# Seven normalisations: halves added on GpSimd, mean squares by token on the partitions

## The chip, the cores and the metric

The kernel runs on one core of one Trainium2 chip. A core has TensorE (PE, matrix products into the 8 banks of PSUM; its weight loads are listed apart as PEld), VectorE (DVE), ScalarE (ACT), GpSimd (POOL) and the DMA queues, SyncE's (SP) among them. Each engine works through its own queue in order; they meet through semaphores. The metric is the device time of one execution in microseconds; lower is better. All data are fp32.

## The reference

One pass over x of shape (4, 256, 32, 32): a convolutional gate, windowed attention, then two layers of fast weights, a pattern layer, head-mixing attention and a mixture of experts, on 4096 tokens of 256 channels. Between them stands this, seven times in what runs here:

```python
def layer_norm(x, g, b):
    m = jnp.mean(x, axis=-1, keepdims=True)
    v = jnp.mean(jnp.square(x - m), axis=-1, keepdims=True)
    return (x - m) * jax.lax.rsqrt(v + EPS) * g + b
```

`_ln_t` is the same without g and b. The axis is that of the 256 channels; EPS is 1e-5.

## The kernel before

The program is a row of stages; each is a block with one instruction stream for each engine and ends in a barrier of all engines (end_stage). Activations lie channels on partitions: a tensor of [128, 2, 4096], where the 2 (CH) are the halves of the 256 channels and 4096 (T) the tokens. So a mean over channels is a sum over partitions, which PE does with a matrix of 1/256 ("ones"), and over two halves.

norm_stage (L338 to L468) runs as ln2, lnf0, lnff, lnf1, ln3, ln4 and ln5, in this order; lnf0, lnff and lnf1 have a gain and a shift. (ln3s stands in a branch of pattern_layer that isn't taken.) It works on NG = 8 groups of GROUP = 512 tokens. For a group g:

- mean(g), L368: two matmuls of 512 columns (one a half) with "ones" into bank g % 3. Every row of the bank then holds the mean.
- centre(g), DVE, L441: dst = src - mean, 128x1024.
- square(g), ACT, L412: squares into sq, three buffers.
- squares(g), PE, L376: two matmuls of 512 columns with a slice of pick, a matrix with one column of 1/256 in it, so that group g's sum falls on row g % 4 of bank 3 or 4. Four groups (HALF) fill a [4, 512] tile.
- root(b), ACT, L416, and invert(b), DVE, L445: square root and reciprocal on [4, 512], once for each half of the groups.
- spread(g), PE, L386: one matmul of 512 columns that takes row g % 4 of rstd to all 128 partitions, bank 5 + g % 3.
- scale(g), DVE: dst times that bank, in one instruction (L451) or, with a gain, in two (L455). move(g), ACT, L424: the shift, two instructions.

The order is written out by hand. PE: means two ahead of squares, groups 0 to 3; then squares of groups 4 to 7, each followed by a spread of groups 0 to 3; then the spreads of 4 to 7. DVE: six centrings, the first reciprocal, two centrings, four scalings, the second reciprocal, four scalings. ACT: five squares, a root, three squares, a root, the shifts. POOL only fills constants (L357 to L360). An fp32 matmul is two MATMUL records in the trace.

The prediction also names rows of other stages: L704 and its neighbours (fast_weight_stage, 32x32 and 128-column tiles), L1755 (matmuls of one moving column), L2119 (of eight), L1215 and L1784 (transposes of 128 columns), L655 and L1692 (additions on POOL), L106 (an activation of one element a partition).

## Time and profile before

| | |
|---|---|
| time, median of 3 runs | 5374.98 us (5358.56 to 5387.59) |
| the profiled execution | 5375.21 us, span 5373.4 us |
| PE busy | 4530.5 us (84%) |
| DVE busy | 2972.1 us (55%) |
| ACT busy | 2152.0 us (40%) |
| POOL busy | 831.7 us (15%) |
| L368, means, PE | 128 records from X and 96 from Y |
| L445, reciprocals of [4, 512], DVE | 14, about 3.34 us each |

The span is from the first to the last instruction that the profile shows; the rest of the time lies around it. Busy shares are averages over stages with different limits, so what a change of one stage is worth is read in that stage. PEclk is the clock that was granted to TensorE, as a share of its full 2.4 GHz; it has two levels, 1.0 and 0.5, and a mean of a window lies between them.

### The profile page before, as it was taken

How to read it: one execution, taken by the hardware profiler on the slowest of the kernel's cores; microseconds unless marked ns; L12 is line 12 of the kernel's file. 1: busy time of each engine (PE TensorE's matmuls, PEld its weight loads, DVE VectorE, ACT ScalarE, POOL GpSimd, SP SyncE). 2: the span in 40 equal slices, each digit the busy share in tenths (PEclk: the TensorE clock that was granted, in tenths of full speed). 3: DMA queues.
4: the chain of work that ended last, by engine and by line, in shares of the span. 5: the costliest groups of instructions: out<-in, count | busy, mean ns of one | idle time of the engine just before them, and what ended most of it. 6: DMA issues, size and time to landing. Idle time of an engine off the chain costs nothing. (4 is left out here: it accounts for less than half of the span.)

```text
span 5373.4 us, 139944 instructions
## 1 busy us (share of the span) xinstructions
PE 4530.5 (84%) x57100; PEld 2834.8 (53%) x57101; DVE 2972.1 (55%) x5849; ACT 2152.0 (40%) x4091; POOL 831.7 (15%) x2139
## 2 busy tenths in 40 slices
PE   3679898887997888897688886799999999984995
PEld 1237777773436777774355554354454545433663
DVE  3444444453024544454488886488686877852343
ACT  1133223232123333331466664277575766721221
POOL 0000000000000000000355553011111111104012
PEclk7788878798998988898899998899999999985997
DMA  1000000000000000000100000000000000006123
GB/s 42 2 7 3 3 3 3 3 3 18 0 0 9 4 3 3 3 4 3 38 1 1 1 1 0 10 1 1 1 0 1 0 1 1 0 3 217 61 84 101
DMA packets 47552, 85.70 MB, mean 16 GB/s; under 512 B 7121, under 2 KB 38129, under 8 KB 46065
## 3 DMA queue, kind: packets, MB, share of 16 engines
q1 hardware_dynamic: 40944, 61.84, 3.3%
q0 software_dynamic: 6144, 16.79, 1.0%
q8 instruction: 401, 6.57, 0.5%
q14 instruction: 63, 0.51, 0.0%
HBM read 45.05 MB, written 33.55 MB: 15 GB/s over the span
## 5 line engine op out<-in xcount | busy, mean ns | idle before, releaser
L1775 PE MATMUL psum<-hm_ex,hm_mix 128*128 128x512 f32 x1024 | 510.4, 621 | 42.3 <-ACT hm_Aq L1855 38.3
L1841 ACT ACTIVATE hm_ex<-psum,hm_nm 128x1024 f32<-128x1024 f32 x256 | 285.6, 1116 | 299.4 <-DVE hm_nm L1899 299.4
L1775 PEld LDWEIGHTS psum<-hm_ex,hm_mix 128*128 128x128 f32 x1024 | 175.6, 191 | 352.5 <-issue 344.8
L1914 DVE COPY hm_A<-psum 128x1024 f32<-128x1024 f32 x256 | 312.9, 1222 | 51.5 <-PE psum L1784 47.9
L1909 DVE TENSOR_SCALAR_CACHE_REDUCE hm_plus<-hm_Aq,hm_cbcol,hm_sums 128x1024 f32<-128x1024 f32 x256 | 340.5, 1330 | 0.0
L1899 DVE TENSOR_REDUCE hm_nm<-psum 128x1 f32<-128x1024 f32 x256 | 311.0, 1215 | 13.5 <-PE psum L1763 13.5
L1784 PEld LDWEIGHTS psum<-K,hm_Aq 128*128 128x128 f32 x2048 | 236.6, 140 | 150.0 <-issue 145.4
L957 DVE TENSOR_TENSOR fw_M<-fw_M,psum 128x256 f32<-128x256 f32 x256 | 107.8, 421 | 348.1 <-PE psum L728 345.6
L1846 ACT ACTIVATE hm_junk<-hm_Aq 128x1024 f32<-128x1024 f32 x256 | 270.6, 1057 | 30.3
L1763 PE MATMUL psum<-hm_kt,hm_qd 64*32 64x512 f32 x4096 | 280.1, 606 | 0.0
L1321 ACT ACTIVATE pt_signs<-pt_acts,pt_tb 128x1024 f32<-128x1024 f32 (+1 forms) x224 | 227.6, 1018 | 116.1 <-POOL pt_tb L1188 95.0
L1784 PE MATMUL psum<-K,hm_Aq 128*128 128x128 f32 x2048 | 266.6, 273 | 5.7 <-DVE hm_A L1914 5.6
L1855 ACT ACTIVATE hm_Aq<-psum 128x1024 f32<-128x1024 f32 x256 | 259.5, 1014 | 11.1 <-PE psum L1775 11.1
L704 PE MATMUL psum<-fw_rk,fw_ntx 128*128 128x64 f32 x2048 | 253.9, 278 | 0.0
L704 PEld LDWEIGHTS psum<-fw_rk,fw_ntx 128*128 128x128 f32 x2048 | 247.4, 194 | 6.7
L715 PE MATMUL psum<-fw_M,fw_pkt 128*32 128x128 f32 x1024 | 185.2, 310 | 74.3 <-issue 38.1
L669 PE MATMUL psum<-fw_w,fw_stage 128*128 128x512 f32 (+1 forms) x512 | 226.6, 593 | 22.9 <-POOL fw_stage L650 19.0
L655 POOL TENSOR_TENSOR fw_loff<-fw_bg,K 128x256 f32<-128x256 f32 x64 | 57.0, 890 | 1163.2 <-DVEq L937 1163.2
L1235 PE MATMUL psum<-pt_w_proc,pt_keptT 128*128 128x512 f32 x512 | 225.6, 599 | 10.3 <-ACT pt_keptT L1306 10.3
L2226 ACT ACTIVATE ex_ht<-psum,ex_b 128x128 f32<-128x128 f32 x320 | 91.2, 368 | 324.6 <-PE psum L2158 241.6
L1692 POOL TENSOR_TENSOR hm_mix<-hm_kron,hm_rinv 128x128 f32<-128x128 f32 x256 | 102.1, 399 | 664.8 <-DVE hm_rinv L1904 664.8
L1405 DVE TENSOR_SCALAR_CACHE_REDUCE pt_over<-pt_acts,pt_tb 128x1024 f32<-128x1024 f32 (+1 forms) x96 | 101.7, 1097 | 161.9 <-POOL pt_tb L1188 161.9
(379 smaller groups left out, 9044.6 us busy)
## 6 DMA issues: line engine op xcount, KB each, us to landing
ex_rows_in<-ex_zero SPq DMA_DIRECT2D x2, 5120.0 KB, 24.8
ex_xs<-ex_rows_in SPq DMA_DIRECT2D x80, 128.0 KB
ex_rows_out<-ex_ys SPq DMA_DIRECT2D x80, 128.0 KB, 1.7
ex_w<-in_ex_w SPq DMA_DIRECT2D x2, 4096.0 KB
X<-in_x SPq DMA_DIRECT2D x2, 2048.0 KB, 12.5
out_y<-X SPq DMA_DIRECT2D x2, 2048.0 KB, 9.0
ff_w<-in_ff_w SPq DMA_DIRECT2D x2, 1024.0 KB, 5.8
pt_w_proc<-in_pt_proc SPq DMA_DIRECT2D x1, 2048.0 KB, 7.6
```

The source lines that it names most:

```text
L669: mm = pe.matmul(bank[b][:, 0:hi - lo], stage[:, h, :], w[:, h, lo:hi], start=(h == 0), stop=(h == CH - 1))
L704: mm = pe.matmul(bank[2][:, 64 * n:64 * n + 64], by[:, n, :], of(n), start=True, stop=True)
L1321: act.activation(signs[:, u, 0:n], acts[:, lane(j), u, 0:n], ACT.Sign, bias=tb[:, lane(j), u, 0:1], accum_out=tb[:, lane(j), u, 1:2]).then ...
L1763: mm = pe.matmul(bank[2 * u + c][32 * pr:32 * pr + 32, :], qd[64 * c:64 * c + 64, u, pr, :, :].rearrange("p j n -> p (j n)"), kt[64 * c:64 ...
L1775: mm = pe.matmul(bank[4 + c], mix[:, u, :], ex[:, u, 512 * c:512 * c + 512], start=True, stop=True)
L1784: mm = pe.transpose(bank[6 + m // 4][:, P * (m % 4):P * (m % 4) + P], Aq[:, u, P * m:P * m + P], k.const("ident"))
L1841: act.activation(ex[:, u, :], flat2(psum[:, 2 * u:2 * u + 2, :]), ACT.Exp, bias=nm[:, u:u + 1], accum_out=rsum[:, u:u + 1]).then_inc(s_ex, 1)
L1846: act.activation(junk[:, :], Aq[:, u, :], ACT.Square, accum_out=ssq[:, bass.ds(b * TI + i, 1)]).then_inc(s_sq, 1)
L1855: act.activation(Aq[:, u, :], flat2(psum[:, 4:6, :]), ACT.Copy).then_inc(s_cp, 1)
L1899: dve.tensor_reduce(nm[:, u:u + 1], flat2(psum[:, 2 * u:2 * u + 2, :]), AX.X, ALU.max, negate=True).then_inc(s_nm, 1)
L1909: dve.tensor_scalar(plus[:, :], Aq[:, u, :], cbcol[:, :], sums[:, :], ALU.add, ALU.add, accum_out=sums[:, :]).then_inc(s_run, 1)
L1914: dve.tensor_copy(A[:, :, :, QT_ * t:QT_ * t + QT_], flat2(psum[:, 6:8, :]).rearrange("p (m g n) -> p m g n", m=MT, g=HEADS)).then_inc(s_a ...
```

## The change

POOL now adds the two halves of the channels before PE sums over partitions: halves(g) = src[0] + src[1], two buffers, so that mean(g) is one matmul of 512 columns; and sqs(g) = sq[0] + sq[1], two buffers. The mean squares are then taken with the tokens on the partitions: four matmuls a group, each with 128 tokens of sqs as the stationary operand and one column of "ones" moving, give a [128, 4] tile in bank 3 + g % 2. Root and reciprocal work on [128, 4], once for each group. spread(g) is four matmuls with one column of rstd, read 128 times, as the stationary operand, and the identity (128 columns) moving; each gives 128 of the group's 512 columns. pick is gone. The order is one loop over t on each engine: PE mean(t), squares(t-2), spread(t-3); ACT square(t), root(t-2), move(t-4); DVE centre(t), invert(t-2), scale(t-3); POOL sum_halves(t+2), sum_squares(t). New waits: mean on halves, squares on sqs and std, square on sqs (two buffers of sq instead of three), root on its own group's squares, invert on its own group's root; scale waits for square(g).

```diff
@@ -338,67 +338,79 @@
 def norm_stage(k, name, src, dst, gain=None, shift=None):
     nc = k.nc
-    HALF = NG // 2
+    PARTS = GROUP // P
     with ExitStack() as ctx:
-        sq = k.sb(f"{name}_sq", [P, 3, CH, GROUP], ctx)
-        std = k.sb(f"{name}_std", [HALF, 2, GROUP], ctx)
-        rstd = k.sb(f"{name}_rstd", [HALF, 2, GROUP], ctx)
-        eps = k.sb(f"{name}_eps", [P, 1], ctx)
-        pick = k.sb(f"{name}_pick", [P, 2 * HALF - 1], ctx)
-        s_zero, s_eps, s_mean, s_cen, s_sq, s_msq, s_std, s_rstd, s_bc, s_out, s_shift = (
-            k.sem(f"s_{name}_{n}") for n in "zero eps mean cen sq msq std rstd bc out shift".split())
+        sb = lambda n, s: k.sb(f"{name}_{n}", s, ctx)
+        halves = sb("halves", [P, 2, GROUP])
+        sq = sb("sq", [P, 2, CH, GROUP])
+        sqs = sb("sqs", [P, 2, GROUP])
+        std = sb("std", [P, NG, PARTS])
+        rstd = sb("rstd", [P, NG, PARTS])
+        eps = sb("eps", [P, 1])
+        s_eps, s_halves, s_mean, s_cen, s_sq, s_sqs, s_msq, s_std, s_rstd, s_bc, s_out, s_shift = (
+            k.sem(f"s_{name}_{n}") for n in "eps halves mean cen sq sqs msq std rstd bc out shift".split())
         bank = k.bank
         at = lambda ap, g: ap[:, :, GROUP * g:GROUP * g + GROUP]
         both = lambda ap: ap.unsqueeze(1).broadcast_to([P, CH, GROUP])
         with nc.Block() as block:
             @block.gpsimd
             def _(pool):
-                pool.memset(eps[:, :], EPS)
-                pool.memset(pick[:, :], 0.0).then_inc(s_zero, 1)
-                pool.wait_ge(s_zero, 1)
-                pool.memset(pick[:, HALF - 1:HALF], 1.0 / C).then_inc(s_eps, 1)
+                def sum_halves(g):
+                    if g >= 2:
+                        pool.wait_ge(s_mean, g - 1)
+                    pool.tensor_tensor(halves[:, g % 2, :], at(src, g)[:, 0, :], at(src, g)[:, 1, :],
+                                       ALU.add).then_inc(s_halves, 1)
+                def sum_squares(g):
+                    pool.wait_ge(s_sq, g + 1)
+                    if g >= 2:
+                        pool.wait_ge(s_msq, g - 1)
+                    pool.tensor_tensor(sqs[:, g % 2, :], sq[:, g % 2, 0, :], sq[:, g % 2, 1, :],
+                                       ALU.add).then_inc(s_sqs, 1)
+                pool.memset(eps[:, :], EPS).then_inc(s_eps, 1)
+                sum_halves(0)
+                sum_halves(1)
+                for g in range(NG):
+                    if g + 2 < NG:
+                        sum_halves(g + 2)
+                    sum_squares(g)
             @block.tensor
             def _(pe):
                 def mean(g):
+                    pe.wait_ge(s_halves, g + 1)
                     if g >= 3:
                         pe.wait_ge(s_cen, g - 2)
-                    for h in range(CH):
-                        mm = pe.matmul(bank[g % 3], k.const("ones"), src[:, h, GROUP * g:GROUP * g + GROUP],
-                                       start=(h == 0), stop=(h == CH - 1))
-                    mm.then_inc(s_mean, 1)
+                    pe.matmul(bank[g % 3], k.const("ones"), halves[:, g % 2, :], start=True, stop=True).then_inc(s_mean, 1)
                 def squares(g):
-                    pe.wait_ge(s_sq, g + 1)
-                    r = g % HALF
-                    for h in range(CH):
-                        mm = pe.matmul(bank[3 + g // HALF][0:HALF, :], pick[:, HALF - 1 - r:2 * HALF - 1 - r],
-                                       sq[:, g % 3, h, :], start=(r == 0 and h == 0),
-                                       stop=(r == HALF - 1 and h == CH - 1))
+                    pe.wait_ge(s_sqs, g + 1)
+                    if g >= 2:
+                        pe.wait_ge(s_std, g - 1)
+                    for q in range(PARTS):
+                        mm = pe.matmul(bank[3 + g % 2][:, q:q + 1], sqs[:, g % 2, P * q:P * q + P], k.const("ones")[:, 0:1],
+                                       start=True, stop=True)
                     mm.then_inc(s_msq, 1)
                 def spread(g):
-                    pe.wait_ge(s_rstd, g // HALF + 1)
+                    pe.wait_ge(s_rstd, g + 1)
                     if g >= 3:
                         pe.wait_ge(s_out, g - 2)
-                    r = g % HALF
-                    pe.matmul(bank[5 + g % 3], k.const("ident")[0:HALF, r:r + 1].broadcast_to([HALF, P]),
-                              rstd[:, g // HALF, :], start=True, stop=True).then_inc(s_bc, 1)
-
-                mean(0)
-                mean(1)
-                pe.wait_ge(s_eps, 1)
-                for g in range(HALF):
-                    mean(g + 2)
-                    squares(g)
-                mean(6)
-                mean(7)
-                for g in range(HALF):
-                    squares(HALF + g)
-                    spread(g)
-                for g in range(HALF):
-                    spread(HALF + g)
+                    for q in range(PARTS):
+                        mm = pe.matmul(bank[5 + g % 3][:, P * q:P * q + P], rstd[:, g, q:q + 1].broadcast_to([P, P]),
+                                       k.const("ident"), start=True, stop=True)
+                    mm.then_inc(s_bc, 1)
+                for t in range(NG + 3):
+                    if t < NG:
+                        mean(t)
+                    if 0 <= t - 2 < NG:
+                        squares(t - 2)
+                    if 0 <= t - 3 < NG:
+                        spread(t - 3)
             @block.scalar
             def _(act):
@@ -407,14 +419,13 @@
                 def square(g):
                     act.wait_ge(s_cen, g + 1)
-                    if g >= 3:
-                        act.wait_ge(s_msq, g - 2)
-                    act.activation(sq[:, g % 3, :, :], at(dst, g), ACT.Square).then_inc(s_sq, 1)
-
-                def root(b):
-                    act.wait_ge(s_msq, HALF * b + HALF)
-                    act.activation(std[:, b, :], bank[3 + b][0:HALF, :], ACT.Sqrt,
-                                   bias=eps[0:HALF, :]).then_inc(s_std, 1)
+                    if g >= 2:
+                        act.wait_ge(s_sqs, g - 1)
+                    act.activation(sq[:, g % 2, :, :], at(dst, g), ACT.Square).then_inc(s_sq, 1)
+                def root(g):
+                    act.wait_ge(s_msq, g + 1)
+                    act.activation(std[:, g, :], bank[3 + g % 2][:, 0:PARTS], ACT.Sqrt, bias=eps[:, :]).then_inc(s_std, 1)
                 def move(g):
                     if shift is not None:
@@ -423,14 +434,13 @@
                             to = at(dst, g)[:, h, :]
                             act.activation(to, to, ACT.Identity, bias=k.vec(shift, h)).then_inc(s_shift, 1)
-                for g in range(HALF + 1):
-                    square(g)
-                root(0)
-                for g in range(HALF + 1, NG):
-                    square(g)
-                root(1)
-                for g in range(NG):
-                    move(g)
+                for t in range(NG + 4):
+                    if t < NG:
+                        square(t)
+                    if 0 <= t - 2 < NG:
+                        root(t - 2)
+                    if 0 <= t - 4 < NG:
+                        move(t - 4)
                 if shift is not None:
                     act.wait_ge(s_shift, NG * CH)
@@ -440,13 +450,13 @@
                     dve.wait_ge(s_mean, g + 1)
                     dve.tensor_tensor(at(dst, g), at(src, g), both(bank[g % 3]), ALU.subtract).then_inc(s_cen, 1)
-                def invert(b):
-                    dve.wait_ge(s_std, b + 1)
-                    dve.reciprocal(rstd[:, b, :], std[:, b, :]).then_inc(s_rstd, 1)
+                def invert(g):
+                    dve.wait_ge(s_std, g + 1)
+                    dve.reciprocal(rstd[:, g, :], std[:, g, :]).then_inc(s_rstd, 1)
                 def scale(g):
                     dve.wait_ge(s_bc, g + 1)
-                    dve.wait_ge(s_cen, g + 1)
+                    dve.wait_ge(s_sq, g + 1)
                     if gain is None:
                         dve.tensor_tensor(at(dst, g), at(dst, g), both(bank[5 + g % 3]), ALU.mult).then_inc(s_out, 1)
                     else:
@@ -455,16 +465,13 @@
                             last = dve.scalar_tensor_tensor(to, to, k.vec(gain, h), bank[5 + g % 3], ALU.mult, ALU.mult)
                         last.then_inc(s_out, 1)
-                for g in range(HALF + 2):
-                    centre(g)
-                invert(0)
-                centre(6)
-                centre(7)
-                for g in range(HALF):
-                    scale(g)
-                invert(1)
-                for g in range(HALF, NG):
-                    scale(g)
+                for t in range(NG + 3):
+                    if t < NG:
+                        centre(t)
+                    if 0 <= t - 2 < NG:
+                        invert(t - 2)
+                    if 0 <= t - 3 < NG:
+                        scale(t - 3)
                 dve.wait_ge(s_out, NG)
```

## Rows read from the trace of the kernel before

**Rows 1.** Timeline, first and last instruction of ln2, lnf0, ln5: start us, us, engine, line.

```profile
198.01 0.10 POOL L357 MEMSET ln_eps<- 128x1 f32 x1 [197.55 <-POOLq L98]
...
245.94 1.22 DVE L451 TENSOR_TENSOR H<-H,psum 128x1024 f32<-128x1024 f32 x1 [0.49 <-PE psum L386]
...
282.35 0.10 POOL L357 MEMSET lnf_eps<- 128x1 f32 x1 [84.05 <-POOLq L98]
...
329.25 1.33 ACT L424 ACTIVATE H<-H,V 128x512 f32<-128x512 f32 x2 [0.37 <-DVE H L455]
...
4790.04 0.10 POOL L357 MEMSET ln_eps<- 128x1 f32 x1 [60.60 <-POOLq L98]
...
4835.32 1.22 DVE L451 TENSOR_TENSOR H<-H,psum 128x1024 f32<-128x1024 f32 x1 [0.48 <-PE psum L386]
```

**Rows 2.** Timeline, one period of the first half of ln2.

```profile
207.84 1.98 PE L368 MATMUL psum<-X,K 128*128 128x512 f32 x4
...
209.75 1.88 PE L376 MATMUL psum<-ln_sq,ln_pick 128*4 128x512 f32 x4
...
209.86 1.22 DVE L441 TENSOR_TENSOR H<-X,psum 128x1024 f32<-128x1024 f32 x1 [2.50 <-PE psum L368]
...
211.11 1.06 ACT L412 ACTIVATE ln_sq<-H 128x1024 f32<-128x1024 f32 x1 [2.67 <-DVE H L441]
```

**Rows 3.** Timeline, the last half of ln2 begins.

```profile
235.33 3.33 DVE L445 RECIPROCAL ln_rstd<-ln_std 4x512 f32<-4x512 f32 x1
238.72 3.77 PE L386 MATMUL psum<-ln_rstd,K 4*128 4x512 f32 x4 [4.57 <-DVE ln_rstd L445]
```

**Rows 4.** Windows, ln2: stretch, us, busy PE PEld DVE ACT POOL (count), PEclk, DMA, GB/s.

```profile
198.00:204.00 6.00, 5.95 (x8) 2.62 (x9) 1.22 (x1) 1.04 (x2) 0.23 (x3) 0.55 0.00 0
204.00:238.00 34.00, 30.16 (x65) 7.32 (x63) 19.11 (x13) 8.86 (x10) 0.00 (x0) 0.99 0.00 0
238.00:246.00 8.00, 7.19 (x8) 2.46 (x8) 4.38 (x5) 0.00 (x0) 0.00 (x0) 0.50 0.00 0
```

**Rows 5.** Groups by line: busy us, mean ns of one, idle before.

```profile
L412 ACT ACTIVATE ln_sq<-H 128x1024 f32<-128x1024 f32 x32 | 33.7, 1055 | 57.9 <-DVE H L441 57.7
...
L451 DVE TENSOR_TENSOR H<-H,psum 128x1024 f32<-128x1024 f32 x32 | 39.1, 1221 | 35.1 <-PE psum L386 35.1
...
L455 DVE SCALAR_TENSOR_TENSOR H<-H,V,psum 128x512 f32<-128x512 f32 x48 | 33.7, 744 | 23.0 <-PE psum L386 23.0
...
L1904 DVE RECIPROCAL hm_rinv<-hm_rsum 128x1 f32<-128x1 f32 x256 | 42.1, 164 | 9.2 <-ACT hm_ex L1841 5.1
```

**Rows 6.** Single lines: min/median/max ns, first and last start.

```profile
L106 ACT ACTIVATE warm<-K x10: 202/203/204, 198.0 to 4790.1; 128x1 f32<-128x1 f32 x10
...
L386 PEld LDWEIGHTS psum<-ln_rstd,K x64: 180/234/333, 224.5 to 4833.4; 4*128 4x128 f32 x64
```

**Rows 7.** Timeline, PE: groups of narrow and of 128-column matmuls elsewhere in the kernel.

```profile
2602.81 3.65 PE L1215 MATMUL psum<-K,pt_acts 128*128 128x128 f32 x16 [17.29 <-DVE pt_acts L1433]
...
3467.69 4.96 PE L1755 MATMUL psum<-K,hm_v 128*128 128x1 f32 x32 [0.57 <-DVE hm_v L1944]
...
3500.27 1.04 PE L1784 MATMUL psum<-K,hm_Aq 128*128 128x128 f32 x8
...
4840.77 27.47 PE L2119 MATMUL psum<-ex_wg,H 128*128 128x8 f32 x128 [5.49 <-DMA ex_before<-in_ex_before]
```

**Rows 8.** Windows: the first fast-weight stage, L1755, L2119; columns as in rows 4.

```profile
343.00:1218.00 875.00, 771.91 (x19644) 630.25 (x19645) 413.20 (x1038) 264.83 (x669) 40.62 (x63) 0.83 0.01 3
...
3467.00:3472.00 5.00, 4.43 (x38) 4.31 (x30) 1.77 (x2) 1.21 (x2) 0.00 (x0) 0.80 0.00 0
4840.80:4868.00 27.20, 27.20 (x128) 27.20 (x129) 7.63 (x39) 0.31 (x1) 0.00 (x0) 0.50 1.04 347
```

**Rows 9.** Groups by line: additions on POOL.

```profile
L1692 POOL TENSOR_TENSOR hm_mix<-hm_kron,hm_rinv 128x128 f32<-128x128 f32 x256 | 102.1, 399 | 664.8 <-DVE hm_rinv L1904 664.8
...
L655 POOL TENSOR_TENSOR fw_loff<-fw_bg,K 128x256 f32<-128x256 f32 x64 | 57.0, 890 | 1163.2 <-DVEq L937 1163.2
```

## The prediction

> **What bounds the kernel now.** The page's share of busy time says PE, but the change touches seven runs of one stage, so I read those alone. First the timeline at their edges: ln2 lasts from 198.01 to 247.16 us (49.2), lnf0 from 282.35 to 330.58 (48.2), ln5 from 4790.04 to 4836.54 (46.5) [rows 1]. ln3 and ln4 are of ln2's kind (they begin with a cold TensorE), lnff and lnf1 of lnf0's (they have a gain and a shift). All seven: 3 x 49.2 + 46.5 + 3 x 48.2 = 338.7 us, 6.3% of the span; nothing overlaps them, since each stage ends in a barrier, so a microsecond saved in a stage is one saved in the time.
>
> Second, the timeline inside one. In the first half PE passes from L368 to L376 and back with hardly a hole, one group of 512 tokens in about 3.7 us, while DVE waits 2.50 us for each mean and ACT 2.67 us for each centring [rows 2]: PE is the bound, through 512-column matmuls. One fp32 matmul is two records of 0.43 us, and the group's five matmuls (two means, two squares, one spread) are 4.3 us. Third, the turn of the halves: the second reciprocal (4 x 512) takes 3.33 us with PE idle, and then the four last spreads run with records about 0.85 us apart [rows 3]. The windows say why: the granted clock is 0.99 while PE is dense, and 0.50 (1.2 GHz) after that idle stretch; at the start of ln2 it is 0.55 [rows 4].
>
> **The change part by part.** PE work of a group. Mean: one matmul instead of two, 2 records: 0.86 us at 2.4 GHz, 1.71 at 1.2 GHz. Squares: four matmuls with sqs as the 128x128 stationary operand and one moving column, 8 records. Such records are 27.47 / 128 = 0.215 us apart at low clock (L2119), and L1755, 32 in 4.96 us across a change of clock, is 0.155 on average [rows 7]; I take 0.11 at high clock, the step of the 128-column records below. 0.9 and 1.7 us. Spread: four matmuls of 128 columns, 8 records: L1784 has 8 in 1.04 us at high clock (0.11 each and a tail), L1215 16 in 3.65 at low clock (0.21 and a tail) [rows 7]: 0.9 and 1.7 us. Three group starts at 0.1 us each. So a group costs PE 2.95 us at high and 5.45 us at low clock, against 4.3 now.
>
> DVE and ACT work. In the new loop DVE does centre(t), invert(t-2), scale(t-3), and invert(t-2) waits for root(t-2), which stands on ACT behind square(t), which waits for centre(t). That is a new wait, and queued behind it are the scaling and the next centring. The ring: centre 1.22 [rows 2], hand-over 0.1, square 1.06 [rows 5], root of 4 columns 0.2 (the nearest is the 1-column activation of 0.203 [rows 6]), hand-over 0.1, reciprocal of 4 columns 0.17 (one column takes 0.164 [rows 5]), scale 1.22 [rows 5], less 0.07 of overlap = 4.0 us a group. With gain, two operations of 0.744 [rows 5], less the same overlap, are 1.4: 4.2. The two reciprocals of 3.33 us a stage go, and with them the halt at the middle; 8 x 0.17 us takes their place. So at high clock the ring of 4.0 or 4.2 us is the bound and hides PE; at low clock PE's 5.45 is the bound and hides the ring.
>
> POOL. Two additions of 128x512 a group, which nothing in the trace shows at that size. Nearest: 128x128 in 0.399 and 128x256 in 0.890 us [rows 9]; a line through them gives 1.9 for 512, and at the other end stands something over twice the smaller one, 1.0. I take 1.5, between them. Two a group are 2.0 to 3.8 us, hidden in every period; what shows is the entry. POOL cannot be the bound unless an addition takes over 2 us. The Trainium skill speaks against the move: "GPSIMD Engine Reference", section 3.1 (Elementwise), has a two-input fp32 add of 2048 elements at 4497 ns, twice VectorE's, and calls the engine wrong for such work. Its figures make 512 elements about 1.24 us as an estimate, 2.5 a group, and the sum would be some 6 us lower than by my 1.5; no run so far shows it.
>
> Entry. halves(0) ends at 1.6 us, mean(0) is read at 2.8, centre(0) ends 4.1, square(0) 5.3, POOL (busy with halves(1) and (2) to 4.6) has sqs(0) at 6.9 and halves(3) at 8.4, so centre(3) starts at 9.8 us. The old stage needed nothing before its first mean; the new start is the slower one, and the periods after it must pay for it.
>
> Stage at high clock: 9.8 + 4 periods of 4.0 to centre(7) = 25.8; then centre, square, root and invert 2.8, four scalings 4.8 and 0.9 of waiting for the last squares = 34.3 us. With gain and shift: 9.8 + 16.8 + 2.8 + 5.6 + 0.9 and the last two shifts 1.4 = 37.3. Stage at low clock, by PE: 2.5 us of waiting in the entry, 8 x 5.45, then 0.4 to the reader and the last scaling 1.2 = 47.7; with gain and shift 49.2.
>
> **Which clock?** This decides it. Narrow matmuls do not lift the clock: L2119 kept PE busy for all of 27.20 us and the granted clock stayed 0.50; in L1755 PE was busy 4.43 of 5 us and the mean clock was down to 0.80 [rows 8]. Dense wide ones did lift it: 0.55 in the first 6 us of ln2, 0.99 after [rows 4]. The new stage is half of each: mean and spread stand next to each other (spread(t-3), mean(t+1)), with the squares between. The nearest mixture in this kernel is the fast-weight stage, 32- to 128-column groups among 512-column ones: clock 0.83 [rows 8], that is two thirds of the time high. The entry with its lone means is sparser than that. I take 0.6 high. Plain: 0.6 x 34.3 + 0.4 x 47.7 = 39.7. Gain and shift: 0.6 x 37.3 + 0.4 x 49.2 = 42.1. Seven: 4 x 39.7 + 3 x 42.1 = 285.1, against 338.7: -53.6 us. From the profiled execution's 5375.2 (span 5373.4 and 1.8 around it; the median of the runs is 5375.0) this gives 5322 us. The next stages began at low clock before, and will again; I put nothing there.
>
> **The rivals.** *High clock throughout:* the ring sets all. 4 x 34.3 + 3 x 37.3 = 249.1, -90: 5286 us. For it: two thirds high in the mixture above. Against: idle entry, narrow squares.
> *Low clock throughout:* 4 x 47.7 + 3 x 49.2 = 338.4, no change: 5375 us. A wait of PE on DVE is exchanged for slow matmuls. For it: L1755 and L2119. Three stages start low. The skill has a case of this kind ("TensorE: Matmul & The Clock Gate", section A second HAM failure mode): small idle gaps between groups made the clock swing back and forth and cost throughput; that would put us between this and the forecast. The trace has it too, 0.83 in the fast-weight stage [rows 8].
> *Slower:* spread's stationary operand is one column read 128 times. The only such load in the trace is L386's, with 180/234/333 ns at least, median and most [rows 6], now hidden under 512 columns. Were each of the 8 loads 0.333 us and no longer covered, at low clock a group costs 8 x 0.12 = 1.0 us more, 7.7 a stage, 54 over seven: 5429 us. It decides from a step of 0.27 us a record (+27 us). Against: its 4x128 form was loaded in 180 ns as well, no more than others.
> *Additions at 1.9 us or 1.0:* entry 1.6 us later or 2 earlier, +11 or -14 us on the forecast; they stay hidden otherwise.
>
> **How the numbers follow.** Forecast (mixed clock) 0.65, its own range with a share high of 0.35 to 0.85 and both ends of POOL's price 5295 to 5352; high throughout 0.10; low throughout 0.16; slower 0.06; 0.03 for something else (another rounding could set pattern_layer's flag, and ln3s and search_stage would run too, hundreds of us). The range reaches from below the high-clock case to above the low-clock one: 5278 to 5380. A change under 0.5% (27 us) can't be told from none here. Faster by more: 0.65 less 0.05 for its slow edge, and 0.10 = 0.70. Same: 0.05 + 0.16 = 0.21. Slower: 0.09.
>
> **What would show it.** Right: stages of 38 to 44 us; no reciprocal over 0.3 us; periods of 4.0 us where the clock is 1.0 and about 5.4 where it is 0.5; DVE waiting for root(t-2) at high clock and for the spread at low. POOL's additions between 1.0 and 1.9 us, nobody waiting for them after the entry. Wrong: spread records over 0.25 us apart at low clock, PE waiting for sqs or halves in mid-stage, a clock of 0.50 through all seven, or a search stage in the trace.

## The result, and where the time went

The changed kernel takes 5447.57 us (median of 4 runs, 5409.84 to 5462.49) beside 5367.02 us (5358.56 to 5387.59) of the kernel before: ratio 1.014, 95% interval 1.011 to 1.018. It is slower by about 80 us. The profiled execution took 5461.57 us, with a span of 5459.8. All ratios here are of fast executions alone; two were slow, the profiled one of a_pad (5364.42 us) and one of a_170 (17363.64 us).

First the page of the changed kernel, parts 1 and 3 (busy time of each engine, DMA queues):

```profile
PE 4614.6 (85%) x57548; PEld 3043.3 (56%) x57549; DVE 2932.5 (54%) x5891; ACT 2156.4 (39%) x4133; POOL 967.7 (18%) x2237
...
q8 instruction: 409, 6.70, 0.5%
```

PE is busy for 84 us more than before, though it has less to do in the seven stages. POOL has 136 us more. Queue q8, by which instructions reach the engines, brought 401 packets before:

```profile
q8 instruction: 401, 6.57, 0.5%
```

Next, windows of the changed kernel, with the columns of [rows 4]: ln2, lnf0, then the first and the second fast-weight stage.

```profile
198.20:236.40 38.20, 30.89 (x144) 23.61 (x144) 20.10 (x24) 9.96 (x17) 20.03 (x17) 0.75 0.00 0
271.90:312.70 40.80, 32.47 (x144) 25.40 (x144) 21.87 (x32) 20.20 (x33) 20.07 (x17) 0.75 0.00 1
...
313.20:1260.90 947.70, 838.09 (x19968) 682.77 (x19968) 422.02 (x1060) 268.48 (x674) 46.56 (x70) 0.77 0.01 4
1618.10:2582.50 964.40, 849.51 (x19968) 689.32 (x19968) 421.97 (x1060) 268.45 (x674) 46.62 (x70) 0.75 0.01 4
```

And the two fast-weight stages of the kernel before, whose code the change does not touch:

```profile
331.50:1240.40 908.90, 792.24 (x19968) 643.48 (x19968) 422.30 (x1060) 267.44 (x674) 46.46 (x70) 0.83 0.01 4
1614.30:2467.80 853.50, 744.63 (x19968) 608.23 (x19968) 422.15 (x1060) 266.89 (x674) 46.50 (x70) 0.88 0.02 4
```

The norm stages (first to last instruction) take 38.2, 40.8, 40.8, 39.1, 38.8, 38.2 and 39.5 us in their order, 275.4 together; before they took 341.1 (49.6 for ln2, 48.6 for lnf0, 47.0 for ln5). Both count the waits at a stage's end too, which [rows 1] leave out (49.2 for ln2). That is -65.7. The two fast-weight stages went from 908.9 + 853.5 to 947.7 + 964.4, +149.7. Everything else together moved by 2.4. The sum is the 86.4 us between the spans.

The window rows say more. The two stages' length less PE's busy time is 225.5 us before (116.7 + 108.9) and 224.5 after (109.6 + 114.9), with 19968 MATMUL records a stage in both. PE isn't idle for longer. The same records take longer, since the granted clock fell from 0.83 and 0.88 to 0.77 and 0.75.

Inside ln2, groups by line of the changed kernel (busy us, mean ns of one, idle before), where [rows 3, 5, 6, 9] stood:

```profile
L370 POOL TENSOR_TENSOR ln_sqs<-ln_sq 128x512 f32<-128x512 f32 x8 | 10.2, 1273 | 8.3 <-ACT ln_sq L424 8.3
L363 POOL TENSOR_TENSOR ln_halves<-X 128x512 f32<-128x512 f32 x8 | 10.1, 1271 | 2.0 <-PE psum L387 2.0
...
L428 ACT ACTIVATE ln_std<-psum,ln_eps 128x4 f32<-128x4 f32 x8 | 1.9, 250 | 3.7 <-PE psum L394 3.7
L455 DVE RECIPROCAL ln_rstd<-ln_std 128x4 f32<-128x4 f32 x8 | 1.4, 176 | 8.2 <-ACT ln_std L428 8.2
```

One period there at high clock (timeline; compare [rows 2]):

```profile
213.75 1.22 DVE L451 TENSOR_TENSOR H<-X,psum 128x1024 f32<-128x1024 f32 x1 [0.49 <-PE psum L387]
...
215.01 1.06 ACT L424 ACTIVATE ln_sq<-H 128x1024 f32<-128x1024 f32 x1 [3.91 <-DVE H L451]
...
215.97 0.25 ACT L428 ACTIVATE ln_std<-psum,ln_eps 128x4 f32<-128x4 f32 x1
...
216.25 0.18 DVE L455 RECIPROCAL ln_rstd<-ln_std 128x4 f32<-128x4 f32 x1 [1.28 <-ACT ln_std L428]
...
216.34 1.21 DVE L461 TENSOR_TENSOR H<-H,psum 128x1024 f32<-128x1024 f32 x1
...
217.47 1.21 DVE L451 TENSOR_TENSOR H<-X,psum 128x1024 f32<-128x1024 f32 x1
```

The centrings start at 213.75 and 217.47: 3.72 us a group, through square, root, reciprocal and scaling. The reciprocals of [rows 3] are gone. And two scalings in ln5 at a clock of 0.50 (timeline, DVE), 5.12 us apart, each waiting for the spread:

```profile
4899.82 1.22 DVE L461 TENSOR_TENSOR H<-H,psum 128x1024 f32<-128x1024 f32 x1 [0.74 <-PE psum L403]
...
4904.94 1.22 DVE L461 TENSOR_TENSOR H<-H,psum 128x1024 f32<-128x1024 f32 x1 [0.74 <-PE psum L403]
```

So the stages did what was forecast. What has to be explained is why a change in one stage slows another one.

**Where PE stops.** The timeline of PE in the second fast-weight stage of the kernel before has one halt in each iteration of the loop whose releaser is "issue", which is to say nothing that the profile shows:

```profile
1846.58 0.42 PE L736 MATMUL psum<-fw_intra,fw_U 128*32 128x128 f32 x7
1848.22 0.51 PE L736 MATMUL psum<-fw_intra,fw_U 128*32 128x128 f32 x9 [1.23 <-issue]
...
1870.39 0.62 PE L736 MATMUL psum<-fw_intra,fw_U 128*32 128x128 f32 x11
1872.33 0.42 PE L736 MATMUL psum<-fw_intra,fw_U 128*32 128x128 f32 x5 [1.31 <-issue]
...
1894.44 0.64 PE L736 MATMUL psum<-fw_intra,fw_U 128*32 128x128 f32 x15
1896.19 0.30 PE L736 MATMUL psum<-fw_intra,fw_U 128*32 128x128 f32 x1 [1.11 <-issue]
```

L736 is a run of 16 records. The halt lies behind 7, 11 and 15 of them, 9, 5 and 1 before the end. It moves by 4 records from one iteration to the next. These are the tenth to twelfth iteration. The same ones in the changed kernel (L735 there is L728 of before, another run of 16, and L743 is L736):

```profile
1862.13 0.32 PE L735 MATMUL psum<-fw_U,fw_kk 32*32 32x32 f32 x15 [1.59 <-issue]
...
1892.18 0.31 PE L735 MATMUL psum<-fw_U,fw_kk 32*32 32x32 f32 x11 [1.27 <-issue]
...
1922.85 0.26 PE L735 MATMUL psum<-fw_U,fw_kk 32*32 32x32 f32 x7 [1.48 <-issue]
```

Here the halt lies before the last 15, 11 and 7 records of L735, with the whole 16 of L743 still to come: 31, 27 and 23 records before the end. That is 22 records earlier in the code every time. Each record has a weight load beside it, so it is 44 instructions. Counted in PE's compiled instruction stream, the loop of the second fast-weight stage begins at instruction 20775 before and at 21331 after, which is 556 = 2 x 256 + 44 further on; the first one's went from 4869 to 5147, 256 + 22. A packet of q8 has 16384 bytes (6.57 MB in 401), and an instruction of the stream 64 bytes: 256 a packet. So the halts go with fixed places of the stream, at a period of 256 instructions, and the longer norm stages (139 more PE instructions in each) have pushed the loops' code past them.

The loop is not unrolled as a whole. PE's code for a stage is a loop of 5095 instructions, four iterations written out, that runs six times, with a few single ones ahead of it and behind it. At each of its five jumps back PE halts for longer, in the kernel before too (timeline, PE):

```profile
1922.23 1.05 PE L715 MATMUL psum<-fw_M,fw_pkt 128*32 128x128 f32 x4 [3.45 <-issue]
```

**What PE waits for there.** The trace has the start and the duration of every packet of q8. Beside the ends of five halts, in us:

| kernel, halt | packet starts | has landed | PE goes on | after landing |
|---|---|---|---|---|
| before, L736 | 1845.75 | 1846.67 | 1848.22 | 1.55 |
| before, L736 | 1869.65 | 1871.11 | 1872.33 | 1.22 |
| before, jump back, L715 | 1919.24 | 1920.47 | 1922.23 | 1.76 |
| after, L735 | 1859.64 | 1860.62 | 1862.13 | 1.51 |
| after, L735 | 1920.31 | 1921.46 | 1922.85 | 1.39 |

All traces of this case say the same. Laid beside PE's compiled stream record by record (its 197 entries that are labels of branches not counted), the 14 traces have 590 halts of over 0.6 us with "issue" in the fast-weight stages, jumps back aside ("common halts" below). All 590 end at places 194 to 196 modulo 256, and all 590 end 1.2 to 1.7 us after a packet of 16384 bytes has landed. Packets come only every 5 us or so, which makes chance a poor explanation. The 140 jumps back halt PE for 2.6 to 4.7 us and end 1.6 to 2.3 us after a landing. So PE halts because it has run out of instructions.

Iterations as windows, two of before (the second has the jump back at 1922.23) and two of after:

```profile
1864.00:1888.00 24.00, 20.94 (x643) 17.18 (x635) 13.16 (x33) 8.33 (x21) 1.34 (x2) 1.00 0.02 3
...
1911.80:1942.40 30.60, 26.88 (x641) 22.04 (x631) 13.13 (x33) 8.28 (x21) 1.34 (x2) 0.72 0.01 3
```

```profile
1854.20:1884.40 30.20, 27.68 (x649) 22.52 (x638) 13.15 (x34) 8.40 (x21) 1.34 (x2) 0.72 0.01 3
...
1914.60:1945.20 30.60, 27.86 (x637) 22.46 (x628) 13.11 (x33) 8.29 (x21) 1.34 (x2) 0.72 0.01 3
```

An iteration with a halt takes 23.6 to 24.2 us before where the clock stays at 1.0, and 30.2 to 30.6 in these windows of after where it falls to a mean of 0.72. Of 62 iterations (from one reduction into fw_sm to the next) 30 keep a granted clock of 1.0 before, and 9 after. The ten with a jump back lose it in both kernels. Of those with a common halt, 23 of 42 keep it before and 1 of 41 after. The halt itself is there in both kernels and costs about the same (1.1 to 1.3 and 1.3 to 1.6 us in the rows above). What differs is how often the clock falls.

### The profile page after: what moved, and what is told of

It is laid out like the page before. It is cut to its first block and busy times, and to the rows that moved or that the text cites. A ratio compares the mean times of both kernels' runs of the same rounds, so it can differ in the third digit from the quotient of the medians.

```text
span 5459.8 us, 141148 instructions
## 1 busy us (share of the span) xinstructions
PE 4614.6 (85%) x57548; PEld 3043.3 (56%) x57549; DVE 2932.5 (54%) x5891; ACT 2156.4 (39%) x4133; POOL 967.7 (18%) x2237
## 5 line engine op out<-in xcount | busy, mean ns | idle before, releaser
L676 PE MATMUL psum<-fw_w,fw_stage 128*128 128x512 f32 (+1 forms) x512 | 256.8, 657 | 22.4 <-POOL fw_stage L657 19.1
L722 PE MATMUL psum<-fw_M,fw_pkt 128*32 128x128 f32 x1024 | 205.9, 337 | 70.0 <-DVE fw_M L995 33.9
L711 PE MATMUL psum<-fw_r,fw_ntx 128*128 128x64 f32 x1024 | 211.7, 392 | 0.6 <-ACT fw_r L854 0.6
```

The lines of the kernel that those rows point to most:

```text
L676: mm = pe.matmul(bank[b][:, 0:hi - lo], stage[:, h, :], w[:, h, lo:hi], start=(h == 0), stop=(h == CH - 1))
L711: mm = pe.matmul(bank[2][:, 64 * n:64 * n + 64], by[:, n, :], of(n), start=True, stop=True)
```

## The experiments

To move code and change nothing else, waits that are already met were put into PE's queue: at the end of conv_stage, ahead of everything here, and in some kernels in ffn_stage, between the two fast-weight stages. Two such waits make one instruction, with at most one instruction more at the end of conv_stage. "Place" is how much further the loops' code stands than in the kernel before, first and second stage, modulo 256. "Halts" are those of over 0.6 us with "issue" in the six rounds of the two loops, 48 iterations, jumps back aside. Lengths, clocks and iterations of the two fast-weight stages, one profiled execution each:

| kernel | place | the two stages, us | clocks | halts | iterations at 1.0, of 62 | ratio to before (95%) |
|---|---|---|---|---|---|---|
| before | 0, 0 | 908.9 + 853.5 = 1762.4 | 0.83, 0.88 | 43 | 30 | 1 |
| after | 22, 44 | 947.7 + 964.4 = 1912.1 | 0.77, 0.75 | 44 | 9 | 1.014 (1.011 to 1.018) |
| b_pad | 22, 44 | 931.4 + 920.7 = 1852.1 | 0.80, 0.80 | 46 | 18 | 1.017 (1.013 to 1.022) |
| a_pad | 0, 0 | 890.5 + 892.0 = 1782.5 | 0.84, 0.83 | 45 | 29 | 0.992 (0.989 to 0.995) |
| b_late | 0, 0 | 895.0 + 872.4 = 1767.4 | 0.84, 0.85 | 47 | 30 | 1.001 (0.999 to 1.004) |
| b_128 | 128, 128 | 861.1 + 842.2 = 1703.3 | 0.88, 0.89 | 32 | 33 | 0.994 (0.991 to 0.996) |
| b_256 | 0, 0 | 871.9 + 888.1 = 1760.0 | 0.88, 0.83 | 44 | 31 | 1.004 (1.001 to 1.006) |
| b_192 | 192, 192 | 823.5 + 847.1 = 1670.6 | 0.90, 0.87 | 11 | 40 | 0.982 (0.977 to 0.987) |
| b_64 | 64, 64 | 904.4 + 911.4 = 1815.8 | 0.81, 0.82 | 41 | 21 | 1.013 (1.008 to 1.019) |
| a_106 | 128, 150 | 872.4 + 884.5 = 1756.9 | 0.86, 0.84 | 37 | 22 | 0.985 (0.981 to 0.989) |
| a_two | 76, 152 | 863.3 + 876.3 = 1739.6 | 0.87, 0.85 | 27 | 31 | one run, see below |
| a_fill | 86, 172 | 884.2 + 873.5 = 1757.7 | 0.84, 0.86 | 41 | 25 | 0.984 (0.979 to 0.990) |
| a_170 | 192, 214 | 834.7 + 819.1 = 1653.8 | 0.88, 0.90 | 7 | 44 | 0.964 (0.960 to 0.969) |
| a_best | 192, 214 | 819.4 + 817.0 = 1636.4 | 0.90, 0.91 | 7 | 44 | 0.964 (0.961 to 0.967) |

Two things differ from place to place. At 192 (b_192, a_170, a_best) nearly all common halts are gone, 7 to 11 beside 41 to 47 at 0, 64 and 22/44. And where there are as many, another share of the halted iterations loses the clock. The jumps back halt PE for 2.6 to 4.7 us in every kernel. A stage's length in one execution is uncertain: b_late and b_256, both at place 0, have 895.0 + 872.4 and 871.9 + 888.1 where before has 908.9 + 853.5, though the sums lie within 8 us.

Ratios are to the kernel before on the same chip. That matters: the expert stage alone takes about 522 us in some of these traces (before, b_pad, a_best) and 485 in others (b_192, b_64, a_170), chip by chip and whatever the kernel.

### b_pad: the kernel before, its code moved as the change moves it

```diff
+                for _ in range(42):
+                    pe.wait_ge(s_w, 96)
...
+                for _ in range(44):
+                    pe.wait_ge(s_w, 48)
```

> The kernel before, all its stages unchanged, with waits that are long met added to PE's queue where PE idles: 22 more instructions ahead of the first fast-weight stage, 44 more ahead of the second. That brings the loops of these stages to the same place within 256 instructions as in the changed kernel, where the traces showed 39 and 111 us more in them. Theory A (the place of PE's instructions, and with it where the loop stalls for instructions): about +100 to +150 us, the fast-weight stages 940 us and more, the stall moved from L736 to the group before it. Theory B (the norm stages' arithmetic, timing or start times): as before, within 0.5%.

Measured: 5470.58 beside 5376.69 us, 1.017. The norm stages took 340.7 us, as before; the fast-weight stages 89.7 more. The halts stand where the changed kernel has them, record for record (timeline, PE; L732 is L728 of before):

```profile
1888.77 0.32 PE L732 MATMUL psum<-fw_U,fw_kk 32*32 32x32 f32 x15 [1.42 <-issue]
...
1918.94 0.31 PE L732 MATMUL psum<-fw_U,fw_kk 32*32 32x32 f32 x11 [1.35 <-issue]
...
1947.90 0.31 PE L732 MATMUL psum<-fw_U,fw_kk 32*32 32x32 f32 x7 [1.58 <-issue]
```

44 instructions that do nothing make the old kernel slower by 1.7%. This is the main result: a loss doesn't need the new norm stage. Its size is under what was expected: 94 us in the medians, not 100 to 150, and stages of 931 and 921 us, not 940 and more.

### a_pad: the changed kernel, its code moved back to the same places

```diff
+                for _ in range(466):
+                    pe.wait_ge(s_w, 96)
...
+                for _ in range(468):
+                    pe.wait_ge(s_w, 48)
```

> The changed kernel with waits that are long met in PE's queue, 234 instructions at two places where PE idles, so that the fast-weight loops lie 512 and 1024 instructions from their places in the kernel before, the same place within 256. Theory A: the fast-weight stages back at 854 to 910 us, the norm stages stay at 38 to 41, in all about 5300 to 5320 us, 1% faster than before. Theory B: no change from the changed kernel, about 5440.

Measured: 5341.32 us, 0.992. The fast-weight stages fell from 1912.1 to 1782.5. The waits are not free: conv_stage took 190.9 us instead of 179.9, ffn_stage 266.7 instead of 240.9, some 37 together, which is why the time lies above the 5300 to 5320 us expected. Without them the 42 us gained by the ratio would be some 79, and the norm stages' own part is 72.9 (268.2 us). The profiled execution is the longest of the ten, so its stages are rather long. Of its 51 common halts 44 are in L736 of before again.

### b_late: the kernel before, the same code on PE, begun later

```diff
-                dve.wait_ge(s_dch, own.n + 1)
+                own.n += 1
+                own.sync()
+                for _ in range(12):
+                    own.done(dve.memset(ca[:, :, :], 0.0))
```

> The kernel before with 12 memsets chained on DVE at the end of the convolution stage, some 5 us, so that all later stages start later and PE's instructions stay where they are. Theory A: +5 us and no more. Theory B (start times): a change of tens of us in the fast-weight stages.

Measured: 5388.93 us, 1.001 (0.999 to 1.004), 12 us in the medians, of which conv_stage's 7 are the delay. Windows of the two fast-weight stages:

```profile
337.90:1232.90 895.00, 779.91 (x19968) 634.05 (x19968) 422.30 (x1060) 267.69 (x674) 46.57 (x70) 0.84 0.01 4
1606.80:2479.20 872.40, 766.42 (x19968) 626.77 (x19968) 422.18 (x1060) 267.08 (x674) 46.59 (x70) 0.85 0.02 4
```

The first fast-weight stage begins 6.4 us later, and the sum of the two stays (1767.4 beside 1762.4), though how it divides between the two does not. When a stage begins is not what costs 90 us.

### b_128, b_256, b_192, b_64: the kernel before at other places

```diff
+                for _ in range(254):     # b_256: 510, b_192: 382, b_64: 126
+                    pe.wait_ge(s_w, 96)
```

> The kernel before with 128 instructions (waits long met) ahead of both fast-weight stages, half of 256. Theory A: the stall lies elsewhere again, so these stages change by tens of us either way. Theory B: +1 to +7 us for the waits themselves.

> The kernel before with 256 instructions (waits long met) ahead of both fast-weight stages. Theory A, with instructions fetched in blocks of 256 (the trace has packets of 16384 bytes on the instruction queue): the loops keep their place in a block, so as before, plus 0 to 5 us for the waits. Rival (any shift matters, or the waits themselves heal or harm something): a change of over 15 us either way, as b_128 or b_pad had.

> The kernel before with 192 instructions ahead of both fast-weight stages, three quarters of 256. Theory A: the stall falls at a third place in the loop, and the time differs from before by 10 to 100 us, sign open. Rival: +0 to 5 us.

> The kernel before with 64 instructions ahead of both fast-weight stages, the place between b_pad (22 and 44, slower) and b_128 (faster). If the place rules: a time that isn't that of before, within 0.98 and 1.02, and an instruction stall in another group of the loop than L736's and L728's. If it doesn't: 1.000 to 1.002.

b_128 measured 5339.93 us, 0.994. Its halts stand in L700 and L706 (L698 and L704 of before), 17 each. Two in L706, among 64-column matmuls:

```profile
1798.13 1.22 PE L706 MATMUL psum<-fw_rk,fw_ntx 128*128 128x64 f32 x10 [0.96 <-issue]
...
1822.14 1.33 PE L706 MATMUL psum<-fw_rk,fw_ntx 128*128 128x64 f32 x6 [0.86 <-issue]
```

b_256 has the code a whole packet further. If the period is 256 instructions, the halts must be as before and the time longer only by the waits. The halt is back in the same run (group by line, first fast-weight stage; L738 is L736 of before, which had 29.6 us of "issue" there):

```profile
L738 PE MATMUL psum<-fw_intra,fw_U 128*32 128x128 f32 x496 | 30.3, 287 | 28.2 <-issue 28.2
```

The two stages take 1760.0 us beside 1762.4, with 44 halts beside 43. The total missed its expectation of 0 to 5 us: the medians are 20 us apart and the ratio's interval stands for 3 to 34 us. conv_stage's waits are 13 of them (192.8 us beside 179.8); the rest is within the interval. The halts' place shows the period of 256 instructions; the total alone would not.

b_192 measured 5247.60 beside 5338.84 us, 0.982: the old norm stages, and 1.8% gained by instructions that do nothing. Most iterations have no halt of over 0.6 us with "issue". Every fourth has that of the jump back, which all kernels have, and in the second stage a common one beside it (timeline, PE, and then the windows of this iteration and the next):

```profile
1721.75 0.32 PE L730 MATMUL psum<-fw_U,fw_kk 32*32 32x32 f32 x14 [1.49 <-issue]
...
1734.15 1.06 PE L717 MATMUL psum<-fw_M,fw_pkt 128*32 128x128 f32 x4 [3.29 <-issue]
```

```profile
1719.70:1754.50 34.80, 29.96 (x645) 24.51 (x636) 13.24 (x34) 8.28 (x21) 1.34 (x2) 0.66 0.01 3
1754.50:1776.90 22.40, 20.88 (x641) 17.29 (x632) 13.11 (x34) 8.28 (x21) 1.34 (x2) 1.00 0.01 4
```

The iteration with the jump back takes 34.8 us, the next one, without a halt, 22.4 at a clock of 1.00. Four in a row are 102.4 us, as many as the kernel before takes from 1840.2 to 1942.4 (102.2), where three halted iterations kept the clock and only the jump back lost it. But before, such a round is the exception: 19 of its 42 iterations with a common halt lost the clock.

b_64 measured 5408.78 beside 5343.26 us, 1.013. Its halts stand in L725 (L723 of before):

```profile
1849.83 0.23 PE L725 MATMUL psum<-fw_tr,fw_M 32*32 32x32 f32 x4 [1.06 <-issue]
...
1873.89 0.22 PE L725 MATMUL psum<-fw_tr,fw_M 32*32 32x32 f32 x3 [1.18 <-issue]
```

So at four places of the same kernel the fast-weight stages take 1670.6 to 1815.8 us, and at the changed kernel's place 1852.1.

### a_106 and a_170: the changed kernel at other places

```diff
+                for _ in range(210):     # a_170: 338
+                    pe.wait_ge(s_w, 96)
```

> The changed kernel with 106 instructions (waits long met) in PE's queue at the end of the convolution stage, where PE idles. The first fast-weight loop then lies 128 instructions (within 256) from its place in the kernel before, where b_128 had 861 and 842 us for the two stages, the second 150. Theory A (place of PE's instructions): norm stages 38 to 41 us as in the changed kernel, fast-weight stages under 880, in all 5270 to 5310 us, the fastest of all. Theory B (the changed norm stages disturb what follows by their timing): over 5340 us.

> The changed kernel with 170 instructions (waits long met) in PE's queue at the end of the convolution stage. The first fast-weight loop then lies 192 instructions (within 256) from its place in the kernel before, where b_192 had 823 us, the second 214. If the place rules: fast-weight stages about 825 and 850 us, norm stages 38 to 41, 60 to 70 us below b_192's ratio of 0.982, that is 0.970 of before. If the changed norm stages harm what follows: 0.985 or more, as a_106.

a_106 measured 5262.18 beside 5338.84 us, 0.985 (5270 to 5310 expected, the second fast-weight stage has 884.5, not under 880). The norm stages give 271.5 us, the fast-weight stages 1756.9, near the 1762.4 of before: the medians' -77 us are the norm stages' -70 and little else. a_170 measured 5159.85 beside 5343.26 us, 0.964, the best here: -183 us in the medians, of which the norm stages' -72.6 (268.5) and the fast-weight stages' -108.6 (1653.8) are 181. That is below the 0.970 expected.

### a_two and a_fill: what the halves on POOL cost

Both leave the rest of the new stage as it is. a_two takes the means by two matmuls as before and has no halves on POOL. a_fill keeps the halves and adds one matmul a group that nobody reads.

```diff
-                    pe.wait_ge(s_halves, g + 1)
...
+                    for h in range(CH):
+                        mm = pe.matmul(bank[g % 3], k.const("ones"), at(src, g)[:, h, :], start=(h == 0), stop=(h == CH - 1))
```

> The changed kernel with the means as before: two matmuls of 512 columns a group, no halves on POOL. It asks what POOL's halves cost or give. By the terms of the prediction: the entry is shorter by some 3 us (no addition before the first mean), PE's group costs 0.86 us more at high and 1.7 at low clock, 3.8 and 7.1 us, and PE streams wide columns more of the time. If the clock stays high for that: norm stages 34 to 37 us. If it falls all the same, PE's 7.1 us a group shows: 42 us and more. The fast-weight loops move too, so only the norm stages are compared.

```diff
+                    pe.matmul(bank[3 + g % 2][:, 8:GROUP], k.const("ones"), at(src, g)[:, 0, 8:GROUP], start=True, stop=True)
```

> The changed kernel with one more matmul of 504 columns beside each mean, into columns of bank 3 or 4 that nothing reads; nothing is left out. It asks whether the clock or PE's work bounds the new norm stage: PE has 0.86 us more a group at high clock and 1.7 at low. If the clock stays up for it: granted clock over 0.88 in the norm stages (0.75 in the changed kernel) and 34 to 38 us a stage, shorter although PE does more. If it doesn't: 45 us and more. The first fast-weight loop lies at 86 of 256, the second at 172, so the total is open by some 50 us either way.

a_two took 9594.68 us, for a reason that isn't the speed of its norm stage: pattern_layer's flag was set, most likely by another rounding of the sums, and search_stage ran for 4332 us (group by line):

```profile
L1593 DVE MAX8 ps_best<-ps_left 128x8 f32<-128x1024 f32 (+1 forms) x1184 | 1334.3, 1127 | 41.0
```

The total is of no use; the stages before it are. ln2, as a window:

```profile
196.00:230.20 34.20, 31.14 (x160) 21.56 (x160) 19.82 (x24) 9.99 (x17) 10.27 (x9) 0.92 0.00 0
```

And ln2 of a_fill, which measured 5258.41 beside 5343.26 us, 0.984:

```profile
197.60:231.70 34.10, 30.38 (x160) 21.39 (x160) 19.86 (x24) 10.10 (x17) 20.09 (x17) 0.92 0.00 0
```

ln2 takes 34.2 and 34.1 us at a clock of 0.92, beside 38.2 at 0.75 in the changed kernel, and a_fill has all of POOL's additions (20.09 us busy). Its seven stages come to 252.4 us. lnf1 and ln3 have clocks of 0.81 and 0.85 and not the 0.88 expected, and lnf1's 39.2 us is over the 38; the other five have 0.90 to 0.93. More work on PE makes the stages shorter. POOL's additions themselves cost next to nothing (a_two, without the halves, has 34.2 us at the same clock); what they cost is that they take dense work from PE, and with it the clock. As a_fill's code also stands elsewhere, this is read from the stages and not from its ratio.

### a_best: both together

```diff
+                for _ in range(210):
+                    pe.wait_ge(s_w, 96)
...
+                    if name not in ("lnff", "lnf1"):
+                        pe.matmul(bank[3 + g % 2][:, 8:GROUP], k.const("ones"), at(src, g)[:, 0, 8:GROUP], start=True, stop=True)
```

> The changed kernel with a_fill's extra matmul in five of the seven norm stages (not in lnff and lnf1) and 106 instructions (waits long met) in PE's queue at the end of the convolution stage, so that the fast-weight loops lie just where they lie in a_170. If place and clock are the two causes and add up: fast-weight stages 820 to 840 us as in a_170, five norm stages of 34 to 37 us, in all 15 to 25 us below a_170's ratio, 0.960 of before. If the two don't add up: 0.964 or more.

Measured: 5178.63 beside 5372.48 us, 0.964 (0.961 to 0.967). The norm stages are 8.9 us shorter than a_170's (259.6) and the fast-weight stages 17 (1636.4), yet the ratio is the same as a_170's within the intervals, and not the 0.960 expected of two causes that add up. The two can't be told apart; either is 3.6% faster than the kernel before and 5% faster than the change as it was made.

## Why the prediction was wrong, step by step

Forecast: 5322 us, range 5278 to 5380. Measured: 5447.57. The sum over the seven stages was right and on the cautious side; the sentence behind it was not.

- **The stages' gain**, -53.6 forecast, -65.7 measured. The ring of DVE and ACT was put at 4.0 us a group and is 3.72: neighbours on one engine overlap by about 0.1 us (the reciprocal starts at 216.25 and takes 0.18, the scaling starts at 216.34), which I had once and not three times, and the two hand-overs between engines take 0.03 to 0.04 us, not 0.1. Low clock was put at 5.45 and is 5.12 (1.71 for the mean, 1.57 for the squares, 1.84 for the spread, and none of the three starts of 0.1 that I added). The root takes 0.25 us (0.2 assumed), the reciprocal 0.18 (0.17).
- **POOL's addition**: 1.5 us assumed, 1.27 measured, well inside the ends of 1.0 and 1.9. By the Trainium skill, "GPSIMD Engine Reference", section 3.1 (Elementwise), it was 1.24 as an estimate, and the trace agrees. Its verdict that the engine is wrong for such work doesn't decide here, where the additions are hidden. The fourth centring starts 10.5 us into ln2 (9.8 forecast).
- **The clock**: a share of 0.6 high assumed, a mean clock of 0.80; measured 0.75 in ln2, a share of 0.5, and 0.69 to 0.75 in the others. Too high, and made up for by periods that were too long. At a clock of 0.92 a_fill's ln2 takes 34.1 us, where the high-clock rival had 34.3 for 1.0.
- **The broadcast loads** of the slower rival are not dear: a spread's 8 records span 1.14 us at high clock, and at low clock the mean behind them starts 1.84 us after their first (4902.85 and 4904.69 us), 0.23 each, where the rival needed more than 0.27. The outcome was slower, but not by that mechanism.
- **The step that failed**: "The next stages began at low clock before, and will again; I put nothing there." The stages after a norm stage were taken to be independent of it, but for the clock at their start. They share one more thing with it: PE's instruction stream. The term that I put at nothing is +149.7 us. The trace of before had the sign of it: PE's "issue" of 29.6 us at L736 stood in it for the first fast-weight stage, 25 halts of about 1.2 us, and 38.1 us at L715, nearly all of it the jumps back, on the page itself. I never asked what sets their place.
- **The other outcome** named at 0.03, another rounding that sets the flag, came in a_two, as it seems, and not in the change.

What is shown: moving code alone makes a loss of this kind (b_pad) and, with the new stage, takes it back (a_pad, a_106, a_170); the period is 256 instructions (b_256, the 22 records, and the places 194 to 196 of all 590 halts); PE halts for packets of its instructions (each halt ends 1.2 to 1.7 us after a landing); the starting time is not it (b_late).

Two things stay open. One is why a halt of the same length lets the clock stay at 1.0 in one run of matmuls and not in another. At L736 of before the clock stayed for 87 of 167 halts (before, a_pad, b_late, b_256), at L728 of before for 10 of 40 in b_pad and for none of 38 in the changed kernel. The Trainium skill has a related case in "TensorE: Matmul & The Clock Gate", section A second HAM failure mode: micro-idles between groups of matmuls make the clock oscillate, and throughput pays for it. The iterations at 1.00 and 0.72 side by side agree with that, but neither tells which place is a bad one. The other is size: b_pad, at the same places and with as many halts, has 1852.1 us in these stages and the changed kernel 1912.1. By the ratios it is 94 us beside 142 (the 77 of the total and the 65.7 that the norm stages gave). So some 50 to 60 us of the 150 are not reproduced by the place of PE's loops alone. In the changed kernel the code of DVE, ACT and POOL has moved too, by instructions that no run moves by themselves; against this as the cause stands a_pad, which has them moved as well and 1782.5 us.

## What to carry to other kernels

Where a kernel has long loop bodies on TensorE (here 5095 instructions), any edit ahead of them moves their code, and the time of untouched stages can move by more than the edit is worth: here from -92 to +90 us by instructions that do nothing. So compare stage by stage before judging an edit, look for "issue" halts in the untouched stages, and if the halts have moved, try the edit at two or three other places of the stream. And work taken off TensorE is no gain where it isn't the bound and its clock falls for want of it: one extra wide matmul a group made this stage 4 us shorter.

## What the runs showed of the hardware

- PE's instructions arrive in packets of 16384 bytes, 256 instructions. In these loops PE often halts for 0.6 to 2.8 us (median 1.2), always at place 194 to 196 modulo 256 and until 1.2 to 1.7 us after a packet has landed (590 halts in 14 traces); most packets cost nothing that shows.
- A jump back in a loop of 5095 instructions halts PE for 2.6 to 4.7 us (140 jumps, mean 3.5), in every kernel here. All 140 iterations with one lost the clock and took 29.8 to 34.9 us, mean 32.0.
- The other iterations, over all 14 traces: 22.4 us in the mean with no halt and a clock of 1.0 (224 of them), 23.7 with a halt and the clock kept (183), 28.0 with a halt and the clock fallen (256, from 21.0 to 31.3). In 65 more, most of them at a stage's start, the clock was below 1.0 without such a halt.
- Over five places, of 22/44, 64, 128, 192 and 0 modulo 256, the old kernel's two fast-weight stages took 1852, 1816, 1703, 1671 and 1762 us.
- Waits already met are two to an instruction. In a_pad they cost about 0.055 us each in ffn_stage (25.8 us for 468) and half of that in conv_stage (11 us for 466); 254 of them in conv_stage cost 0.8 us (b_128) and 510 cost 13 (b_256).
- A dense filler matmul of 504 columns beside each mean raised the granted clock of ln2 from 0.75 to 0.92.
